# Softmax sums from a column of ones, and three pieces of work moved between engines, in an attention and expert kernel on one Trainium2 core

## The reference

```python
h = _layernorm(x, axis=-1) * (1 + ca) + sa
Q, K, V = h @ Wq + bq, h @ Wk + bk, h @ Wv + bv          # 16 heads of 8
scores = Q @ K.T / sqrt(8) + einsum('bhid,ijd->bhij', Q, rel_emb)
attn = softmax(scores, axis=-1)
x = x + ga * ((attn @ V) @ Wo + bo)                      # ga: one gain per batch and feature
```

## Time and profile before

| | us |
|---|---|
| median of 3 runs (685.5 to 690.84) | 687.17 |
| the profiled execution | 685.29 |
| its span, first to last instruction | 683.6 |
| PE busy | 588.5 (86%) |
| DVE busy | 507.1 (74%) |
| ACT busy | 508.8 (74%) |
| POOL busy | 423.3 (62%) |

### The profile page before, as it was taken

How to read it: one execution, slowest core, us unless ns; L and a number is a source line. 1 busy time by engine, 2 the same in 40 slices (tenths; PEclk the granted TensorE clock), 3 DMA queues, 4 the chain that set the end, 5 groups by cost and what they waited for, 6 DMA issues and landing times. The chain is left out here.

```text
span 683.6 us, 17706 instructions
## 1 busy us (share of the span) xinstructions
PE 588.5 (86%) x5108; PEld 439.8 (64%) x5108; DVE 507.1 (74%) x1888; ACT 508.8 (74%) x1578; POOL 423.3 (62%) x543
## 2 busy tenths in 40 slices
PE   5667789999899899899989989978798989999950
PEld 4444556666666566566666656655577979999940
DVE  6788988999999999999999999997565312222127
ACT  4157799999999999999989999998643434444434
POOL 2660655747668687686776966855366765554535
PEclk9777999999999999999999999999999999999975
DMA  5996678778787788778868878874525777565538
GB/s 142 308 230 202 198 235 248 228 235 248 214 245 241 213 252 246 228 219 260 249 208 242 252 213 247 243 236 148 189 82 174 236 234 228 198 217 185 176 97 274
DMA packets 173125, 149.03 MB, mean 218 GB/s; under 512 B 16182, under 2 KB 162642, under 8 KB 173030
## 3 DMA queue, kind: packets, MB, share of 16 engines
q1 hardware_dynamic: 168054, 139.33, 67.9%
q0 software_dynamic: 4544, 8.44, 3.7%
q10 hardware_dynamic: 432, 0.14, 0.1%
HBM read 83.71 MB, written 65.05 MB: 218 GB/s over the span
## 5 line engine op out<-in xcount | busy, mean ns | idle before, releaser
L711 ACT ACTIVATE P<-NS,nmax 128x256 f32<-128x256 f32 x512 | 254.2, 504 | 50.5 <-DVE nmax L1312 49.6
L1312 DVE CUSTOM_DVE_ANT_0 NS<-psS,bias 128x256 f32<-128x256 f32 x512 | 185.2, 417 | 2.3 <-PE psS L950 1.6
L968 PE MATMUL psT<-ident,P 128*128 128x128 f32 x1024 | 140.0, 281 | 8.9 <-ACT PT L722 8.8
L1267 DVE COPY stage<-psDist 128x768 f32<-128x768 f32 x125 | 118.1, 945 | 33.9 <-issue 25.2
L722 ACT ACTIVATE PT<-psT 128x512 f32<-128x512 f32 x256 | 136.4, 586 | 0.0
L968 PEld LDWEIGHTS psT<-ident,P 128*128 128x128 f32 x1024 | 118.2, 145 | 24.0 <-issue 9.8
L778 ACT ACTIVATE F<-psS,b1T 128x256 f32<-128x256 f32 x156 | 65.4, 471 | 86.5 <-PE psS L1061 86.5
L609 POOL DMA_INDIRECT results_d<-y,row_u x78 | 76.0, 974 | 56.7 <-DVE y L1458 40.8
L711 ACT ACTIVATION_READ_ACCUMULATOR P<-NS,nmax 128x1 f32 x512 | 100.3, 196 | 0.0
L950 PE MATMUL psS<-Kst,Qst 32*128 32x256 f32 x512 | 65.9, 336 | 34.7 <-DVE nmax L1312 29.9
L1061 PE MATMUL psS<-xT,w 128*128 128x256 f32 x312 | 80.6, 381 | 0.3 <-DMA w<-in_L_ffn_w_dram 0.3
(11 more groups left out here) (254 smaller groups left out, 1044.2 us busy)
## 6 DMA issues: line engine op xcount, KB each, us to landing
dist_d<-stage SPq DMA_DIRECT2D x128, 384.0 KB, 3.0
bias<-dist_d SPq DMA_DIRECT2D x256, 192.0 KB, 3.3
w<-in_L_ffn_w_dram SPq DMA_DIRECT2D x39, 512.0 KB, 3.7
x<-slots_d SPq DMA_DIRECT2D x39, 129.0 KB, 3.0
y<-results_d SPq DMA_DIRECT2D x16, 256.0 KB, 5.0
dist_d<-zeros SPq DMA_DIRECT2D x1, 2048.0 KB, 14.4
out_dram<-y SPq DMA_DIRECT2D x8, 256.0 KB, 3.2
results_d<-y,row_u POOLq DMA_INDIRECT x78, 3.0
```

What stands on the lines that cost most here:

```text
L711: act.activation(P[:, p % 2, h, q, :], NS[:, p % 2, h, q, :], ACT.Exp, scale=-1.0, bias=nmax[:, p % 2, k:k + 1], accum_out=lsum[:, b % 2, ...
L968: mm = pe.transpose(psT[:, h, S * k + 128 * q:S * k + 128 * q + 128], P[:, p % 2, h, q, 128 * k:128 * k + 128], ident[:])
L1267: dve.tensor_copy(stage[:, p % STAGES, :, :, :], bank[:, :, 0:2 * RW].rearrange("p h (q c) -> p h q c", q=2)).then_inc(dist_out, 1)
L1312: dve.tensor_tensor_reduce(NS[:, p % 2, h, q, :], psS[:, h, S * q:S * q + S], bias[:, p, h, q, :], 1.0, 3e38, ALU.add, ALU.min, nmax[:, p ...
```

## The change

The value tile gets a column of ones beside each head's eight values (16 columns in place of 8 per head, two heads in 32 columns as four were), so that the product with the probabilities gives the sums too, in both halves of `psO`. After the last product ScalarE copies `psO` to `C`, PE turns it by four transposes back into `psO`, and VectorE takes the inverse of the sums and scales the values, rows on the partitions, in step 4 in place of 3. PE turns the result ("ct") and ScalarE copies it; the output product "y" in step 6 then gives rows at once, with the gain multiplied into `Wo` beforehand ("gain", step 7) and the bias added by a second product. The exponentials have no accumulator. From batch 1 on ScalarE copies the distances in steps 0 and 4. `gather` is one copy for both heads, and `turned` and `pt_done` count once per step. The host puts the rows of `Wo` and `bv` in order.

```diff
+BY_ACT_OUT = (0, 4)
 M_SLOTS = ((("q23", 1),), (("k01", 1),), (("k23", 1),), (("logits", -3), ("v", 1)),
-           (("y", -1), ("nh", 2)), (("u01", -2),), (("u23", -2),), (("q01", 2),))
-X_SLOTS = ((), (("rank", -4),), (("turn", -2),), (("back", -2),), (("tally", 1 - B),), (("rows", -3),), (("t", -1),), ())
+           (("ct", -1), ("nh", 2)), (("u01", -2),), (("u23", -2),), (("q01", 2),))
+X_SLOTS = ((), (("rank", -4),), (("turn", -2),), (("back", -2),), (("gains", 0), ("tally", 1 - B)), (("rows", -3),),
+           (("y", -1),), (("gain", 0),))
...
+def act_puts_out(b, p):
+    return b > 0 and p in BY_ACT_OUT and PAIRS * b + p + AHEAD < STEPS
...
-        V = early("V", [128, 2, JB, HG, 4, HG, D])
+        V = early("V", [128, 2, JB, HG, 4, 2, 2 * D])
...
-            for a in range(4):
-                at = slice(32 * a, 32 * a + 32)
-                sp.dma_start(WoD[at, :], Wo.rearrange("(g a d) e -> a g d e", a=4, d=D)[a]).then_inc(weights_in, 16)
-                sp.dma_start(bvT[at, :], bv.rearrange("(g a d x) -> a g d x", a=4, d=D, x=1)[a],
-                             allow_slow_non_contiguous=True).then_inc(weights_in, 16)
+            sp.dma_start(WoD[:], Wo).then_inc(weights_in, 16)
+            sp.dma_start(bvT[:], bv.rearrange("(e a) -> e a", a=1)).then_inc(weights_in, 16)
...
                     act.activation(P[:, p % 2, h, q, :], NS[:, p % 2, h, q, :], ACT.Exp, scale=-1.0,
-                                   bias=nmax[:, p % 2, k:k + 1],
-                                   accum_out=lsum[:, b % 2, q, a, p // 2:p // 2 + 1]).then_inc(exp_done, 1)
+                                   bias=nmax[:, p % 2, k:k + 1]).then_inc(exp_done, 1)
...
+                act.activation(PT[:, (p // 2) % 2, at:at + 2, :], psT[:], ACT.Copy).then_inc(pt_done, 1)
...
-                    i = act.activation(yT[:], bank[:, 0:S], ACT.Identity, scale=modT[:, 2, b:b + 1],
-                                       bias=gabo[:, b:b + 1])
+                    i = act.activation(ctxT[:], bank[:, 0:S], ACT.Copy)
...
+            def copy_values(b):
+                act.wait_ge(values_done, HG * b + HG)
+                past(act, ctx_full, b)
+                act.activation(C[:], psO[:], ACT.Copy).then_inc(c_copied, 1)
+            def put_out(n):
+                act.wait_ge(dist_done, n + 1)
+                act.wait_ge(written[(n - STAGES) % SLOTS], 16 * ((n - STAGES) // SLOTS) + 16)
+                act.activation(stage[:, n % STAGES, :, :, :],
+                               psD[:, :, 0:2 * RW].rearrange("p h (q c) -> p h q c", q=2), ACT.Copy)\
+                    .then_inc(dist_out, 1)
...
-                    mm = pe.matmul(bank[:, 0:S], WoD[:], ctxT[:], start=True, stop=True)
+                    for k in range(2):
+                        mm = pe.transpose(bank[:, 128 * k:128 * k + 128], ctx_r[:, k, :], ident[:])
...
-                elif name == "t":
-                    pe.wait_ge(m_act, M_TAKEN["y", r][1])
+                elif name == "y":
+                    pe.wait_ge(m_act, M_TAKEN["ct", r][1])
+                    pe.wait_ge(x_dve, X_TAKEN["gain", r][0])
                     for k in range(2):
-                        mm = pe.transpose(spare[:, k, :], yT[:, 128 * k:128 * k + 128], ident[:])
+                        pe.matmul(spare[:, k, :], ctxT[:, 128 * k:128 * k + 128], WoG[:], start=True, stop=False)
+                        mm = pe.matmul(spare[:, k, :], ident[:, r:r + 1].broadcast_to([128, 128]), gR[:, 1, :],
+                                       start=False, stop=True)
+                elif name == "gain":
+                    mm = pe.matmul(spare[:, 0, :], ident[:, r:r + 1].broadcast_to([128, 128]), gR[:, 0, :],
+                                   start=True, stop=True)
...
-                    past(pe, pt_done, 2 * (s - 1) + h + 1)
+                    past(pe, pt_done, s)
...
-                        mm = pe.matmul(psO[32 * a:32 * a + 32, 0:S],
+                        mm = pe.matmul(psO[32 * a:32 * a + 32, S * (g // 2):S * (g // 2) + S],
...
-            def spread_l(b):
-                pe.wait_ge(linv_wide, b + 1)
+            def turn_values(b):
+                pe.wait_ge(c_copied, b + 1)
                 for q in range(2):
-                    mm = pe.transpose(psO[:, S + 128 * q:S + 128 * q + 128],
-                                      linvD[:, q, :, :, :].rearrange("p a g d -> p (a g d)"), ident[:])
+                    for r in range(2):
+                        mm = pe.transpose(psO[:, S * q + 128 * r:S * q + 128 * r + 128],
+                                          C[:, S * r + 128 * q:S * r + 128 * q + 128], ident[:])
                 mm.then_inc(ctx_full, 1)
...
-                    if p == 2:
-                        spread_l(b - 1)
+                if p == 3 and b > 0:
+                    turn_values(b - 1)
...
+            for g in range(HG):
+                i = dve.memset(V[:, :, :, g, :, g % 2, D:D + 1].rearrange("p b k a d -> p (b k) (a d)"), 1.0)
+            i.then_inc(ones_in, 1)
...
             def context(b):
-                dve.wait_ge(lrow_done, b + 1)
+                values = psO[:].rearrange("p (n m d) -> p n m d", n=4, d=2 * D)
+                dve.wait_ge(ctx_full, b + 1)
+                dve.reciprocal(linv[:], values[:, :, :, D:D + 1].rearrange("p n m d -> p n (m d)")).then_inc(linv_done, 1)
                 if b > 0:
-                    dve.wait_ge(m_full, M_FULL["y", b - 1])
-                dve.tensor_tensor(ctxT[:], psO[:, 0:S], lrow[:], ALU.mult).then_inc(ctx_done, 1)
+                    dve.wait_ge(m_full, M_FULL["ct", b - 1])
+                dve.wait_ge(linv_done, b + 1)
+                dve.tensor_tensor(ctx_r[:].rearrange("p q (r m d) -> p (q r) m d", r=2, d=D), values[:, :, :, 0:D],
+                                  rep(linv[:], 3, D), ALU.mult).then_inc(ctx_done, 1)
...
-                if p == 0 and b > 0:
-                    inverses(b - 1)
...
-                if p == 3 and b > 0:
+                if p == 4 and b > 0:
                     context(b - 1)
...
-                if n < STEPS:
+                if n < STEPS and not act_puts_out(b, p):
```

More of the change, by code:

```diff
@@ L56 @@
 X_LATE = ()
-BY_ACT = ("y", "nh", "back")
-M_LAST = (("logits", B - 3), ("y", B - 1), ("u01", B - 2), ("u23", B - 2), ("logits", B - 2), ("u01", B - 1),
+BY_ACT = ("ct", "nh", "back")
+M_LAST = (("logits", B - 3), ("ct", B - 1), ("u01", B - 2), ("u23", B - 2), ("logits", B - 2), ("u01", B - 1),
           ("u23", B - 1), ("logits", B - 1))
-X_LAST = (("turn", B - 2), ("rows", B - 3), ("t", B - 1), ("back", B - 2), ("turn", B - 1), ("rank", B - 3),
+X_LAST = (("turn", B - 2), ("rows", B - 3), ("y", B - 1), ("back", B - 2), ("turn", B - 1), ("rank", B - 3),
           ("rows", B - 2), ("back", B - 1), ("rows", B - 1), ("rank", B - 1))
@@ L73, in list_jobs @@
                     if 0 <= b + shift < B and (name != "rank" or (b + shift) % 2)
-                    and (name != "tally" or b == B - 1)]
+                    and (name != "tally" or b == B - 1) and (name != "gains" or b == 0)]
             done[b, p] = full, dve, act
@@ L241, in attention @@
         nmax = t("nmax", [128, 2, 4])
[L242 to L245, removed]
+        linv = t("linv", [128, 4, 8])
+        C = t("C", [128, 2 * S])
+        ctx_r = t("ctx_r", [128, 2, E])
+        gR = t("gR", [128, 2, E])
+        WoG = t("WoG", [128, E])
         zeros = t("zeros", [128, PITCH - RW])
         ctxT = t("ctxT", [128, S])
-        yT = t("yT", [128, S])
         stats2 = t("stats2", [128, 2, 6])
@@ L709, in exps @@
                     act.wait_ge(max_done, 4 * s + k + 1)
-                    a = 2 * (p % 2) + h
                     act.activation(P[:, p % 2, h, q, :], NS[:, p % 2, h, q, :], ACT.Exp, scale=-1.0,
-                                   bias=nmax[:, p % 2, k:k + 1],
-                                   accum_out=lsum[:, b % 2, q, a, p // 2:p // 2 + 1]).then_inc(exp_done, 1)
+                                   bias=nmax[:, p % 2, k:k + 1]).then_inc(exp_done, 1)
             def gather(b, p):
                 s = PAIRS * b + p
[L718 to L723, removed]
+                act.wait_ge(turned, s + 1)
+                if p % 2 == 0:
+                    past(act, values_done, HG * b + p // 2 - 1)
+                at = 2 * (p % 2)
+                act.activation(PT[:, (p // 2) % 2, at:at + 2, :], psT[:], ACT.Copy).then_inc(pt_done, 1)
             def take(name, b, bank):
@@ L758, in step @@
                     gather(*at)
+                if act_puts_out(b, p):
+                    past(act, x_dve, X_DONE[b, p][1])
+                    past(act, x_act, X_DONE[b, p][2])
+                    put_out(PAIRS * b + p + AHEAD)
                 for name, of in X_OF.get((b, p), ()):
@@ L803, in _ @@
             act.activation(p1[:, 0:1], ident[:, 0:1], ACT.Silu)
-            sums(B - 1)
-            act.wait_ge(m_full, M_FULL["y", B - 1])
-            take("y", B - 1, banks[1])
+            copy_values(B - 1)
```

(12 more changed lines are left out.)

60 lines of the change are left out of this document (23 added, 37 removed).

## The result

The kernel after takes 699.28 us (median of four runs, 695.69 to 703.13) beside 686.34 us of the kernel before on the same chip: ratio 1.0183, 95% interval 1.0104 to 1.0262. The profiled execution took 703.13 us with a span of 701.4, 17.8 more than the 683.6 of before; 703.7 had been predicted.

The account below looks back on a forecast made before the run. PE's chain or VectorE's, whichever is longer, was taken to bound each scores-to-scores interval, ScalarE only some. Terms 5.3 + 8.9 + 3.4 + 1.5 + 0.8 - 1.5 = +18.4 on the profiled 685.29 gave 703.7 us, range 684 to 717.

Parts of the forecast that it names:

- Start: Set-up: eight small loads leave SP's queue, distance-buffer clearing starts sooner, less 0.3 for fills of ones: -1.5 us.
- Moved wait: Step 4: PE's first values product waits 0.85 us for VectorE's scaling; less 0.28 for "ct", +0.57 us per batch.
- Four transposes of the values: Step 3: PE does four transposes where step 2 had two of the inverses; 0 to 0.52, taken as +0.25 us.
- gain: Step 7: VectorE work between its copy and its minima, where scores wait; 0 to 0.48, taken as +0.2 us.
- ScalarE's distances: Step 0: PE's interval falls, -0.17 us; in odd batches from 5 PE's slot product waits for ScalarE's copy, +0.47.
- y: Interval from step 5's scores: eight PE instructions, 0.9 to 1.06 us, replace two transposes; +0.29 odd, +0.04 even batches.
- Exponentials: ScalarE's exponentials without accumulator reads start 0.40 us apart, so a step loses 0.36 us of ScalarE.
- Batch 15 and behind the loop: Batch 15: the same waits without copies, +1.5 us; behind the loop PE's chain carries the last "y", +0.8.
- The last sign: Sign of being right: batches of about 28.4 and 29.8 us in place of 27.0 to 27.3 and 28.6 to 28.9.
- the new waits don't last: Rival, chance 0.19: scaling done when PE arrives, transposes fit into PE's wait in step 3; 13.9 goes: 689.8 us.
- ScalarE is the bound: Rival, chance 0.16: ScalarE, fullest engine, sets the batch; 1.0 us less in each of fifteen batches: -15, 670 us.
- everything adds: Rival, chance 0.10: upper bounds together, stall 1.3, "y" 1.06, exponentials at 0.49, no gain at the start: 715 us.

Follow-up runs that it names:

- b2: Kernel before with Wo and bv loaded by one DMA each instead of four each: 684.5 us, ratio 0.9962.
- e1: Kernel after with VectorE's reciprocal and scaling of the values ahead of the takings of logits and V in step 4: 688.7 us, ratio 1.0041.
- e2: Kernel after with VectorE copying all distances again, no step of ScalarE's: 699.05 us, ratio 1.0194.
- e6: Kernel of e5 with ScalarE copying the distances of step 3 as well as of 0 and 4: 692.84 us, ratio 1.0090.
- b1: Kernel before with the accumulators taken off the exponentials, ones in place of the sums: 692.06 us, ratio 1.0082.
- e5: Kernel of e1 with VectorE's marking of the chosen experts ahead of step 6's distances copy: 684.73 us, ratio 0.9987.
- e4: Kernel after with the accumulators put back on the 512 exponentials, their sums not used: 705.99 us, ratio 1.0295.
- b4: Kernel of b2 with VectorE's cast of the slots behind step 2's distances copy instead of ahead of it: 681.46 us, ratio 0.9949.
- b5: Kernel of b4 with the ranking operations (difference of the logits, marking of chosen experts) moved as in b3: 680.86 us, ratio 0.9923.
- e7: Kernel of e5 with ScalarE copying distances in step 4 alone and the cast of the slots moved as in b4: 687.08 us, ratio 1.0020.
- b3: Kernel of b1 with the difference of the logits moved to step 6's start and the marking ahead of step 6's distances copy: 679.54 us, ratio 0.9916.

## Why the prediction was right

The sum was +18.4 and the traces show +17.8, mostly by the reasons given, partly because errors cancelled, and partly by luck: the medians are only 12.9 apart.

- *Start,* -1.5: measured -1.71, and b2 shows it alone (-2.57).
- *Moved wait,* +0.57 in step 4: +0.56, and e1 takes it away. The product begins 0.82 later behind S; 0.85 had been worked out from VectorE's queue. Two terms of it had no row: the wait behind the reciprocal, put at 0.05, is 0.10 (283.58 to 283.68), and the signal, put at 0.1, is 0.11 (284.10 to 284.21).
- *Four transposes of the values,* +0.25 in step 3: +0.36 from batch 3 on, but -0.14 in batch 2. No run takes them out alone.
- *"gain",* +0.2 in step 7: +0.20 and +0.19; no run takes it out alone.
- *ScalarE's distances,* -0.17 and +0.47 in step 0: -0.18 and +0.51. That they are worth nothing is e2's result.
- *"y":* eight instructions take 0.89, of the 0.9 to 1.06 given. Interval 5 to 6 of slot batches is 3.82 where 3.95 was forecast.
- *Exponentials* 0.40 apart. The group of after (mean 498 ns), then four of them in one row of ScalarE's timeline:

```profile
L704 ACT ACTIVATE P<-NS,nmax 128x256 f32<-128x256 f32 x512 | 218.2, 498 | 78.9 <-DVE nmax L1332 77.3
```

```profile
286.63 1.70 ACT L704 ACTIVATE P<-NS,nmax 128x256 f32<-128x256 f32 x4
```

  (1.70 - 0.50) / 3 is 0.40. The Trainium skill's estimate of 400 ns (ScalarE: Activation LUTs, "What ACT_TABLE_LOAD costs") agrees with this trace.
- *Batch 15 and behind the loop,* +1.5 and +0.8: from S of step 0 in batch 15 to the end of the span it was 224.2 and is 226.6, +2.4. The size fits by luck. "The same waits" are not there: the first values product of batch 15 comes 0.43 after S of step 4.

```profile
491.06 0.50 PE L960 MATMUL psS<-Kst,Qst 32*128 32x256 f32 x4
491.49 1.07 PE L995 MATMUL psO<-PT,V 128*32 128x256 f32 x16
```

  What is longer is S of step 0 to S of step 3 in batch 15, 12.85 beside 10.43, where the granted clock was lower (third from the end), first before, then after:

```profile
459.34:469.77 10.43, 9.13 (x78) 6.13 (x78) 7.59 (x33) 8.81 (x32) 4.56 (x6) 0.84 0.73 214
474.81:487.66 12.85, 11.97 (x76) 7.94 (x76) 6.22 (x30) 9.11 (x18) 5.17 (x6) 0.53 0.70 205
```

  Over all traces this last part takes 224.2 to 229.5, and 224.4 in one with the change (e6) as well as 229.5 in one without it (b1).

The step that failed is the one not taken: VectorE's unedited ranking operations were kept at their lengths. Ranking batches were forecast at +0.04 in step 5 and nothing in step 6; measured -0.54 in four of the six and +0.69 in all. Slot batches had nothing in step 2; measured -0.44. (The forecast also took 4.36 for interval 5 to 6 of all six ranking batches, where 4 and 14 had 3.69 and 3.82.) That each comes from an operation meeting, or no longer meeting, one of GpSimd's is shown for step 6 by e5 and e4, and for step 2 by e2 and, in the kernel before, by b4; for step 5 only the rows say so: in batch 8 before, the difference of the logits (281.77 to 282.86) began inside a product of GpSimd's (281.32 to 282.59), and after it begins 0.48 behind that product's end. b5 doesn't decide it, since it moves the whole operation out of the interval. Against the forecast, over all batches, step 6 makes +4.4, step 5 -2.3 and step 2 -2.2: nothing in the sum, only because they cancel. By groups the sum's terms were less good than the sum: the six ranking batches +8.1 where 5.3 was forecast, the five slot batches +6.7 where 8.9 was, batches 1 to 3 +2.4 where 3.4 was. The last sign, "about 28.4" for the slot batches, doesn't follow from the forecast's own 27.3 + 1.8; they take 28.7.

The rivals: "the new waits don't last" falls with the 0.75 in the row; "ScalarE is the bound" falls with the batches at 29.71 and 28.68 while ScalarE is less busy; "everything adds" would have been 715.

## What to carry to other kernels

When work moves to another place in an in-order queue, work out what stands ahead of it there and who is blocked behind the wait: two lines in another order were worth 10 us here. When an engine gets faster, list which operations on the other engines will now run at the same moment, GpSimd's and VectorE's above all, and take out of the bound any time that comes from their meeting. The release column names the engine that ended last; the program says which wait is meant.

## What was not expected of the hardware

Three of VectorE's operations were held until GpSimd's product was done if GpSimd had started first: the marking and the difference of the logits, each with two inputs from SBUF, and the cast. The marking, 0.22 alone, ended 0.08 after the product (294.15 and 294.07; in b1 287.87 and 287.79), and even the cast, with a single input, took 1.04 in e7. Working from SBUF alone is not enough: a reduction with one input ran its usual 0.21 inside such a product in the kernel after.

```profile
305.41 1.28 POOL L525 TENSOR_TENSOR Qst<-xqk,part 128x512 fp32r<-128x512 f32 x1
...
306.43 0.21 DVE L1398 TENSOR_REDUCE slot_f<-slot_c 128x8 f32<-128x64 f32 x1
```

An operation with one input from PSUM was not held: X from psDist and X took 0.41 in e5 in the middle of GpSimd's product of th and z. Nor was one that started first; in the kernel before the marking began 0.11 ahead of the product:

```profile
286.83 0.21 DVE L1356 TENSOR_TENSOR chosen<-place,places 128x64 f32<-128x64 f32 x1
...
286.94 1.27 POOL L587 TENSOR_TENSOR th<-z,th 128x512 f32<-128x512 f32 x1 [3.69 <-ACT th L737]
```

So whether the marking begins 0.11 ahead of the product or 0.31 behind its start decides over 0.82 us. The Trainium skill (SBUF — State Buffer, "SBUF: two separate sides") describes such a lock: VectorE in a two-port mode, or with two SBUF inputs against a GpSimd instruction that reads SBUF, and GpSimd take the shared pair of ports for a whole instruction, the first to start wins, the other blocks. These traces agree where GpSimd was first; that the cast runs in such a mode no row shows, nor that GpSimd is blocked, since its product took 1.27 behind the marking too. The second surprise is b1's: in three of six batches PE was granted half its clock after standing still for 1.66 us, and in the steady part of no trace after the 0.95 of the kernel after or the 0.92 of b3. There a held VectorE operation was paid for twice.
